# Finishing the tiles of an attention layer inside its edge loop, on one core

## What is computed

```python
edge_index = jnp.stack([src, dst])
x = _layernorm(x + _L0_gnn_ref(x, edge_index, L0_gnn_W, L0_gnn_b), axis=-1)
x = _layernorm(x + _L1_gnn_ref(x, edge_index, edge_weight, L1_gnn_W_rel, L1_gnn_b_rel, L1_gnn_W_root), axis=-1)
x = _layernorm(x + _L2_gnn_ref(x, L2_gnn_W, L2_gnn_att, src, dst), axis=-1)
x = _layernorm(x + _L3_gnn_ref(x, edge_weight, L3_gnn_W, L3_gnn_b, src, dst), axis=-1)
```

```python
# layer 2
z = jnp.einsum('nd,hdf->nhf', h, W)
es = jnp.einsum('nhf,hf->nh', z, a_src)
ed = jnp.einsum('nhf,hf->nh', z, a_dst)
e = jax.nn.leaky_relu(es[src] + ed[dst], SLOPE)
...
ex = jnp.exp(e - m[dst])
denom = jax.ops.segment_sum(ex, dst, num_segments=N)
alpha = ex / safe
out = jax.ops.segment_sum(alpha[:, :, None] * z[src], dst, num_segments=N)
# layer 3
hw = jnp.matmul(h, W)
msg = hw[src] * sym_norm[:, None]
agg = jax.ops.segment_sum(msg, dst, num_segments=n_nodes)
return jax.nn.relu(agg + b)
```

## Time and profile before

| | us |
|---|---|
| median of 3 runs (lowest, highest) | 1610.68 (1608.29, 1614.39) |
| profiled execution: its own time | 1612.43 |
| profiled execution: span of its instructions | 1610.6 |
| TensorE busy | 1435.2 (89%) |
| VectorE busy | 1173.5 (73%) |
| GpSimd busy | 903.0 (56%) |
| ScalarE busy | 489.2 (30%) |
| mean granted TensorE clock | 0.96 of full |

### The profile page before, as it was taken

How to read it: one execution, slowest core, us unless ns; L and a number is a source line. 1 busy time by engine, 2 the same in 40 slices (tenths; PEclk the granted TensorE clock), 3 DMA queues, 4 the chain that set the end, 5 groups by cost and what they waited for, 6 DMA issues and landing times.

```text
span 1610.6 us, 36607 instructions
## 1 busy us (share of the span) xinstructions
PE 1435.2 (89%) x12021; PEld 1158.3 (72%) x12021; DVE 1173.5 (73%) x3010; ACT 489.2 (30%) x910; POOL 903.0 (56%) x909
## 2 busy tenths in 40 slices
PE   4879999999998999999588888888888879999998
PEld 4667778877776888888366666666666657888887
DVE  9788889888853344444599999999999989433443
ACT  0432222222210101003355554555545555100000
POOL 0125654555544556563577777777777710466674
PEclk9989999999999999999598999999999989999999
DMA  5364555545566565541344444444444441756552
GB/s 177 141 205 144 166 164 170 175 143 166 199 218 200 175 207 187 177 138 57 87 112 112 113 112 112 113 113 113 113 112 112 113 153 58 283 193 228 194 154 80
DMA packets 111000, 241.15 MB, mean 150 GB/s; under 512 B 48837, under 2 KB 73641, under 8 KB 104671
## 3 DMA queue, kind: packets, MB, share of 16 engines
q0 software_dynamic: 44832, 128.13, 28.4%
q1 hardware_dynamic: 65983, 110.68, 19.5%
HBM read 192.87 MB, written 50.96 MB: 151 GB/s over the span
## 4 chain that ended last, share of the span: by engine, by line
PE 46%; POOL 19%; issue 14%; DVE 11%; DMA 6%; ACT 1%; DVEq 1%; SPq 1%; POOLq 0%; ACTq 0%
POOL ring L716 16%; PE bank L1769 13%; PE bank L1651 8%; PE bank L1717 5%; PE bank L1696 3%; PE bank L1643 3%; POOL big L671 3%; PE bank L1669 3%; DMA big<-rows_layer,big 2%; PE bank L1901 2%; PE bank L1636 1%; PE bank L1778 1%; DMA ring<-attention_rows,work 1%; DMA big<-edge_weights 1%; PE bank L1576 1%
## 5 line engine op out<-in xcount | busy, mean ns | idle before, releaser
L716 POOL DMA_INDIRECT ring<-attention_rows,work x416 | 394.5, 948 | 147.6 <-issue 143.3
L671 POOL DMA_INDIRECT big<-rows_layer,big x304 | 289.4, 952 | 267.5 <-issue 244.6
L667 POOL DMA_INDIRECT ring<-rows_layer,ring x152 | 151.5, 997 | 171.5 <-PE bank L1696 129.6
L1901 PE MATMUL bank<-work,ring 128*65 128x48 f32 x3328 | 235.3, 231 | 12.2 <-ACT work L892 11.6
L1901 PEld LDWEIGHTS bank<-work,ring 128*65 128x65 f32 x3328 | 224.4, 146 | 21.1 <-ACT work L892 18.5
L892 ACT ACTIVATE work<-work 128x960 f32<-128x960 f32 x84 | 161.8, 1926 | 84.3 <-DVE work L1438 82.3
L1769 PE MATMUL bank<-big,ring 128*128 128x256 f32 x750 | 164.2, 379 | 0.0
L1769 PEld LDWEIGHTS bank<-big,ring 128*128 128x128 f32 x750 | 142.5, 190 | 19.6
L1717 PE MATMUL bank<-big 128*128 128x256 f32 x608 | 140.2, 386 | 9.5 <-DMA big<-rows_layer,big 9.5
L1769 PE MATMUL bank<-big 128*128 128x256 f32 x664 | 145.9, 379 | 0.0
L1769 PEld LDWEIGHTS bank<-big 128*128 128x128 f32 x664 | 126.1, 190 | 17.7 <-ACT big L916 0.4
(11 more groups left out here) (258 smaller groups left out, 2437.8 us busy)
## 6 DMA issues: line engine op xcount, KB each, us to landing
adjacency<-big SPq DMA_DIRECT2D x16, 1600.0 KB, 6.5
big<-adjacency SPq DMA_DIRECT2D x16, 1600.0 KB, 8.0
ring<-adjacency SPq DMA_DIRECT2D x16, 1600.0 KB
ring<-attention_rows,work POOLq DMA_INDIRECT x416
rows_layer<-big SPq DMA_DIRECT2D x50, 128.0 KB, 2.4
edge_rows<-edge_list SPq DMA_DIRECT2D x1, 4983.0 KB
big<-rows_layer,big POOLq DMA_INDIRECT x304, 2.9
rows_layer<-big SPq DMA_DIRECT2D x5, 960.0 KB, 4.3
```

The lines of the kernel that those rows point to most:

```text
L667: G.indirect_dma_start(out=rows0[:, s, :], out_offset=None, in_=y0tab[:, :], in_offset=bass.IndirectOffsetOnAxis(ap=src_l0[j][:, c:c + 1], ...
L671: G.indirect_dma_start(out=rows1[:, s, :], out_offset=None, in_=(y1tab if q < 2 * LAYER else y3tab)[:, :], in_offset=bass.IndirectOffsetOn ...
L716: G.indirect_dma_start(out=rows[0:EP, s, c, 0:ZG], out_offset=None, in_=ztab[:, :], in_offset=bass.IndirectOffsetOnAxis(ap=idx[:, g, c:c + ...
L1901: ins = mm(sum_banks[k % 3][0:FH, h * WIN:(h + 1) * WIN], rows[0:EP, s, c, h * FH:(h + 1) * FH], prob[:, k % 2, c, h * WIN:(h + 1) * WIN], ...
```

## The change

Tile t of layer 2 is complete when its last group has been added. The change computes that group beforehand from the even share of edges (`final_group`), and finishes the tiles 0 to 22 (`EARLY` = 23) inside the loop, in steps that begin three groups after it: at steps 7, 10, 13, 17, 20 and so on to 81, three or four apart. Tiles 23 and 24 are finished behind the loop. If a group after `final_group[t]` should still hold nodes of tile t, one more sweep is made, which finishes all tiles anew.

In the loop the work of a tile is spread over four steps. TensorE: `turn_sums` (four transposes straight from `acc_h`, the staging buffer is gone) ahead of L1867 in the tile's first step, `turn_tile` and `multiply_tile` in the third, the latter behind the sums. VectorE: seven short operations, each placed behind one of the loop's own (`behind`). ScalarE: division in four parts, square root, normalisation, two copies. SP: per tile a store of the normalised rows to a new table in memory (`x3tab`) and one of the product to `y3tab`. One bank (7) serves the tile; it was the third bank of the sums, which now have two. The streams are gone.

Behind the loop SP loads layer 3's products of tiles 0 to 22 back from `y3tab` into `ybuf` (it lies in the memory that the loop's running maxima use), in two parts around the first adjacency load, later the new x of these tiles from `x3tab` into `x_sb`, and only then the fourth adjacency block and the first lists. The dense products take all 400 blocks.

```diff
+    final_group = [int(E * (t + 1) * P / (N * EP * KC) + 0.75) for t in range(NT)]
+    EARLY = sum(g + 6 <= GROUPS for g in final_group)
+    begin = {t: final_group[t] + 3 for t in range(EARLY)}
+    def early(step, age):
+        return [t for t in begin if begin[t] + age == step]
...
 SP, in the loop
+    for t in early(step, 9):
+        sp.wait_ge(n_act, r * (5 * EARLY) + (5 * t + 3))
+        sp.dma_start(x3tab[t * P:(t + 1) * P, :], u2[:, 1]).then_inc(x3_stored, 16)
+    for t in early(step, 10):
+        sp.wait_ge(n_act, r * (5 * EARLY) + (5 * t + 5))
+        sp.dma_start(y3tab[t * P:(t + 1) * P, :], xnT[:, 1].rearrange("p k n -> p (k n)")).then_inc(
 SP, behind the loop
-    for k in range(3):
-        load_a(slots3[k], k, k)
+    load_y3(0, 0, Y_HALF)
+    load_a(slots3[0], 0, 0)
+    load_y3(1, Y_HALF, EARLY)
+    for t in later_tiles:
+        sp.wait_ge(n_act, nsw * (5 * EARLY) + (9 + t - EARLY))
+        sp.dma_start(y3tab[t * P:(t + 1) * P, :], ybuf[:, t, :]).then_inc(rows_stored[2], 16)
+    for k in range(1, 3):
+        load_a(slots3[k], k, k)
+    sp.dma_start(x_sb[:, 0:EARLY, :], x3tab.rearrange("(t p) f -> p t f", p=P)).then_inc(x3_loaded, 16)
+    load_a(slots3[3], 3, 3)
+    lists(after3[3][0])
 ScalarE, in the loop
     for g in range(-2, GROUPS + 1):
+        for t in early(g, 3):
+            multiplied(t)
+        if has(g - 1):
+            rescales(g - 1)
+        for t in early(g, 1):
+            divided(t)
+        for t in early(g, 2):
+            normalised(t)
         if has(g - 1):
             exponentials(g - 1)
         if has(g + 2):
             copy_hots(g + 2)
             penalties(g + 2)
+        for t in early(g, 1):
+            deviation_of(t)
+        for t in early(g, 2):
+            turned(t)
 VectorE, in the loop
+    behind = {masked: (largest_den, 1), new_max: (inverse_den, 1), keep_max: (with_residual, 1),
+              group_max: (tile_stats, 1), rescale: (tile_moments, 1), max_change: (tile_scale, 2),
+              one_hots: (tile_shift, 2)}
 VectorE, the number of sweeps
+    link(V.tensor_tensor(base_f[:], bmin[:], base_f[:], ALU.is_lt))
+    link(V.tensor_reduce(span[:], base_f[:], AX_X, ALU.max))
+    link(V.scalar_tensor_tensor(out=nsw_f[:], in0=nsw_f[:], scalar=1.0, in1=span[:], op0=ALU.add, op1=ALU.add))
 TensorE, in the loop
     for g in range(-2, GROUPS + 1):
+        for t in early(g, 0):
+            turn_sums(t)
         if has(g):
-            stream_to_sums(g)
             transpose_max(g)
         if has(g + 2):
             transpose_hots(g + 2)
+        for t in early(g, 2):
+            turn_tile(t)
         if has(g):
-            stream_to_spread(g)
             spread_max(g)
         if has(g - 1):
             sums(g - 1, range(0, 1))
         if has(g + 2):
             destination_logits(g + 2)
         if has(g - 1):
             sums(g - 1, range(1, H))
+        for t in early(g, 2):
+            multiply_tile(t)
```

More of the change, by code:

```diff
@@ L140, in gnn_program @@
     landed_between = [16 * sum(KC if g < FULL else LAST_CHUNKS for g in range(s, GROUPS, SLOTS)) for s in range(SLOTS)]
+    final_group = [int(E * (t + 1) * P / (N * EP * KC) + 0.75) for t in range(NT)]
+    EARLY = sum(g + 6 <= GROUPS for g in final_group)
+    begin = {t: final_group[t] + 3 for t in range(EARLY)}
+    later_tiles = list(range(EARLY, NT))
+    assert len(later_tiles) == 2 and all(begin[t + 1] >= begin[t] + 3 for t in range(EARLY - 1))
+    def early(step, age):
+        return [t for t in begin if begin[t] + age == step]
     def list_loads(q):
@@ L401, in gnn_program, with free_slots @@
         banks3 = [banks[4], banks[5], banks[2]]
-        blocks3, taken3 = {t: [] for t in range(NT + 3)}, [0] * len(banks3)
-        for step in range(NT + 3):
-            for j, begin in enumerate((5, 8, 12)):
-                while step >= begin and taken3[j] <= step - 5 and len(blocks3[step]) < PAIR:
-                    blocks3[step].append((j, taken3[j]))
-                    taken3[j] += 1
+        y3_loaded = a_stored
+        Y_HALF = NT // 2
         def has(g):
             return 0 <= g < GROUPS
+        def free_slots(r, g):
+            shift = SLOTS - GROUPS % SLOTS if g < GROUPS % SLOTS else 0
+            return r * GROUPS + (g + 1) + ((r > 0) * shift if shift else 0)
         def chunks_of(g):
@@ L639, in _ @@
             G.memset(first_node[:, 0:1], float((NT - 1) * P))
+            first = 0
+            for t in range(EARLY):
+                G.memset(base_f[:, first:final_group[t] + 1], float(t * P))
+                first = final_group[t] + 1
+            G.memset(base_f[:, first:], float(EARLY * P))
             G.iota(steps[:], [[WIN, SWEEPS]], base=WIN, channel_multiplier=0,
@@ new lines, in _ @@
+                    for t in early(g, 2):
+                        turned(t)
+            for j, t in enumerate(later_tiles):
+                act.wait_ge(n_dve, nsw * (7 * EARLY) + (2 + 2 * j))
+                if j:
+                    act.wait_ge(x3_stored, nsw * (16 * EARLY))
+                for h in range(H):
+                    ins = S.activation(u2[:, j, h * F:(h + 1) * F], later_banks[j][:, h * FH:h * FH + F], ACT.Copy,
+                                       scale=dens[j][:, 1, h:h + 1])
+                ins.then_inc(n_act, 1)
@@ L1468, in attention @@
                             part(g + k)
+                        if part in behind:
+                            tile_part, age = behind[part]
+                            for t in early(g, age):
+                                tile_part(t)
             link(V.tensor_copy(base_f[:], bmin[:]))
@@ new lines, in _ @@
+                ins.then_inc(n_pe, 1)
+            for j, t in enumerate(later_tiles):
+                pe.wait_ge(n_act, nsw * (5 * EARLY) + (5 + j))
+                for k in range(2):
+                    ins = T(later_banks[j][:, k * P:(k + 1) * P], x_sb[:, t, k * P:(k + 1) * P], ident[:, :])
+                ins.then_inc(n_pe, 1)
+            for j, t in enumerate(later_tiles):
+                pe.wait_ge(n_act, nsw * (5 * EARLY) + (7 + j))
+                for k in range(2):
+                    ins = mm(later_banks[j][:, D:2 * D], xnT[:, j, k, :], w3_sb[:, k, :], start=(k == 0), stop=(k == 1))
+                ins.then_inc(n_pe, 1)
```

250 lines of the change are left out of this document (144 added, 106 removed).

## The result

| | before | after |
|---|---|---|
| median of 19 runs each, in turn on one chip (lowest, highest), us | 1609.53 (1607.86, 1615.06) | 1616.86 (1607.43, 1633.01) |
| profiled execution: time, span, us | 1612.43, 1610.6 | 1607.43, 1605.6 |
| mean granted TensorE clock | 0.96 | 0.88 |

The ratio is 1.0038 (95% interval 1.0021 to 1.0056): the change makes the kernel a little slower, by about 0.4%. The prediction was 1595 us, 1% faster than before: it had the wrong direction and is 22 us too low, though 1616.86 lies inside its range. The profiled execution of after is the fastest of its 19; a second one, taken later (experiment x0), lasted 1630.3 us.

The account below looks back on a forecast made before the run. GpSimd's gathers were taken to pace the loop, VectorE 0.5 us a group behind. 1610.6 - 31.8 (end of the kernel) + 16 (loop: 9 + 19 - 12) = 1594.8, predicted as 1595 us, range 1578 to 1624.

Parts of the forecast that it names:

- First dense product: Behind the loop: tiles 23 and 24 finished and rows reloaded, so layer 3's first dense product comes 12 us after the loop.
- the 2.5 us for a half clock: At the start of layer 3's dense products: TensorE begins at half clock, which was put at 2.5 us.
- VectorE's work: In the loop: seven operations for each of 23 tiles, 1.14 us a tile after overlap.
- The slack: In the loop: VectorE's 470 us with the tiles against GpSimd's 482 leaves 12 us of slack, subtracted from the loop's costs.
- The clock: In the loop without streams: TensorE's clock low for a quarter of it, a fifth of 96 us paid, 19 us (10 to 45).
- 9 + 19 = 28: In the loop: 9 us for product, turn and late exponential ahead of the transposes, plus 19 us for the low clock.
- The prices for steps that are wholly low: VectorE's stop per wholly low step: 3.0 us with product and turn (14 steps), about 1.75 with one (18), 0.5 otherwise (45).
- The clock falls for good: Rival, 14%: TensorE at half clock for half the loop, 30 low groups at 2.1 us each, 60 us longer, 1639 us.
- Table loads double: Rival, 5%: table loads hold ScalarE twice the measured 1.28 us, stopping VectorE 2 us a tile, 46 us more, 1641 us.
- Larger wait, same mechanism: Rival, 20%: the forecast's mechanism with larger waits, 25 to 40 us in the loop, 1604 to 1619 us.
- The reload is late: Rival, 5%: x and rows going through memory push layer 3's lists and gathers back by 10 us, 1605 us.
- The loop hides all: Rival, 12%: both costs in the loop fit into the slack, 1579 us.

Follow-up runs that it names:

- x0: The changed kernel as it is, run again on the chip of x1 to x3: median 1618.50 us, ratio 1.0044 to the kernel before.
- x1: The kernel before with its five streamed matmuls a group taken out, nothing else: median 1635.96 us, ratio 1.0141 to the kernel before.
- x2: The changed kernel with five streamed matmuls a group put back just ahead of the spread: median 1598.21 us, ratio 0.9923 to the kernel before.
- x6: x2 without streams in the steps that have a tile's turn and product: median 1668.98 us, ratio 1.0350 to the kernel before.
- x8: x2 with the turn of a tile's sums moved behind the transposes, five streams in every step: median 1594.94 us, ratio 0.9895 to the kernel before.
- x3: The changed kernel with the early tiles' square root replaced by the identity, so no table loads in the loop: median 1626.53 us, ratio 1.0096 to before.
- x10: The changed kernel with three streams ahead of the spread in every step: median 1608.17 us, no ratio given.
- x7: x6 with the turn of the sums moved behind the transposes and three streams in that step: median 1631.90 us, ratio 1.0137 to the kernel before.

## Why the prediction was wrong

The steps behind the loop held. First dense product: 12 us after the loop said, 11.3 measured (1355.58). From there to the end 254 said, 250.1 measured; TensorE was at full clock from the first product, so the 2.5 us for a half clock weren't spent. The reload of rows 12 to 22 took 14.6 us from issue to landing instead of 7.7 and some 2, but was wanted only in the middle of the first dense row, and TensorE didn't wait for it. GpSimd's first gather of layer 3 came 38.7 us after the loop ("near 40"), and VectorE waited 10.42 us for x without anyone waiting for it. Gain 36.2 us where 31.8 was said.

The loop failed: 16 us longer said, 32.1 in the fastest execution and about 54 in x0. In the prediction's own terms:

- VectorE's work, 23 x 1.14 = 26 us: 20.2 measured, 0.88 us a tile. Slightly too much.
- **The slack. This is the first step that failed.** 77 x (6.26 - 5.76) = 38.5 us of idle VectorE were taken to be free for work and waits ("12 us of slack stay"). Only waits for gathers can be given back, and these were 31.0 us in the whole loop, of which 6.4 stand in the first 16 us (6.6 after, where 7.9 are left in all): 23.1 were given back. The prediction had the 23.3 us of the earlier trace rows beside it and used the difference of two paces instead. That is 15 us too much.
- **The clock. The second, and the reason behind the slow loops.** "At the half clock the sums and transposes fill the step", said the prediction, and so a quarter of the loop would be low. They did fill it, 34.96 of 36 us above, and the clock stayed low all the same: 0.69 in the loop, where a quarter low would have been 0.87. So 0.62 of the loop was low and not a quarter. Waits for TensorE and ScalarE grew by 35.6 us, where 9 + 19 = 28 were said; in x0 by some 58. The prices for steps that are wholly low were near: 3.0 us where product and turn meet (3.9 in x0, four steps), 1.75 with one of them (2.2 to 2.6 with a product alone, 1.2 with a turn alone), 0.5 elsewhere (0.3; 0.7 in x1). What the prediction had wrong is how much of the loop is low, and on which steps that falls.

So for the fastest execution 20 + 36 - 23 = 33. The median execution is 9.4 us longer than that one; if these are waits of the same kind, as in x0, its loop is some 41 us longer than before where 16 were said: 15 of slack and 17 of waits too little, 6 of VectorE's work too much. That the range held the median is partly luck: these errors and 4 us more gained behind the loop than said work against each other.

x1 and x2 show that the clock hangs on the streams, and not on the tiles: taking the streams from the kernel before costs 23 us with no tile in it, and giving the changed kernel five returns 20 us (1618.50 to 1598.21, on one chip). What the low clock costs is both together: x1, at 0.54 and without a tile, lost 27 us in its loop, x6, at 0.76 with tiles, 96. Not shown is what it is in a stream that keeps the clock, that it fills a pause or that it is a wide matmul: no run filled the pauses with anything else. In the low stretch of 36 us hardly a pause was left, and the clock didn't return. x8's profiled execution is 17.7 us shorter than that of before: 34.1 gained behind the loop, 13.1 lost in it, and 3.3 because its loop began later. The 13.1 are VectorE's work (+19.8) and waits for TensorE and ScalarE (+13) less the gathers (-20.5).

The rivals. *The clock falls for good*: it fell, below the 0.87 at which the rival was to decide, but its price was wrong. Every low group was taken as 8.4 us. Without a product it cost 6.61 (above, and in x1), 0.35 over the gathers' pace and not 2.1; with product and turn it cost 9.8, more than the rival had. *Table loads double*: against it stand the 1.29 us above and x3. *Larger wait, same mechanism*, 25 to 40 us in the loop: this is the case that came, 1604 to 1619, for the profiled execution; x0's loop was longer. *The reload is late*: it isn't. *The loop hides all*: no.

The Trainium skill ("TensorE: Matmul & The Clock Gate", "HAM oscillation — how this bites in real kernels") has the clock swing with waits in every turn of a loop. The trace agrees in part: pauses stand before the falls shown, of 0.3 to 0.9 us, and in x2 the same pauses passed without a fall. The page has the clock come back once the engine is kept busy ("What's actually happening"); here it stayed at half through 36 us of TensorE at 97%, and the measurement decides.

## What to carry to other kernels

Slack is what an engine waits for the thing that sets the pace, read from the chain of waits, and not the difference of two rates; add up what is put on that engine, its own work and its new waits, against it. Work that seems useless may pay for the clock: before taking it out, run the old kernel without it alone. Where work moves into such a loop, find the steps with the heaviest new work on TensorE and see at which clock they run: the same low clock cost 0.35 us in one kind of step and 3.5 in another. Streams in every step kept the clock here; streams chosen so that each step has the same sum of work didn't.

## Unexpected in the hardware

In x1 TensorE stayed at half clock for long, very regular stretches although it was nearly always busy, this one among them:

```profile
865.00:943.00 78.00, 75.66 (x619) 73.06 (x620) 68.36 (x174) 39.02 (x49) 56.47 (x60) 0.50 0.40 107
```

Read in pieces of half a microsecond, five such stretches of 78.5 us began 85 to 86 us apart (864.5, 950, 1035, 1120.5, 1206), with some 7 us between at the higher clock. The clock stayed at half with TensorE busy for 75.66 of 78 us; why it returns for 7 us at such distances, the runs don't show.

The same program scatters very differently from kernel to kernel: the changed one from 1607.43 to 1633.01 us over 19 runs, x10 from 1595.43 to 1628.76, x1 from 1633.10 to 1637.92 and x8 from 1594.71 to 1595.80 over four each. The mean clock of the loop doesn't tell which: x7, at 0.83, stays within 3 us, and x2, at 0.94, has 11. In the changed kernel it is on which steps the low clock falls.
